# A four-layer graph kernel: its last stage with an early first chunk, a table stored by chunk, and a norm that ends in the ring

## Chip, cores and metric

One core of one Trainium2 chip. The metric is the device time of one execution in microseconds, taken as the median over several runs. A difference of 0.2% (5.5 us) is about the smallest that can be told here.

## The reference, cut to what matters

There are 100000 nodes with 32 features each and 25000 edges, sorted by their target `dst`. Four graph layers follow each other, each as `x = layernorm(x + layer(x))`. The last two are a relation layer (RGCN with attention) and a layer of weighted messages:

```python
nei  = segment_sum(a[:, None] * msg, dst)          # layer 3, msg by edge type
curr = h[src[last_e]] @ self_loop_weight
x = layernorm(x + relu(where(in_deg > 0, nei + curr, 0)))
...
messages = x[src] * edge_attr[:, None]             # layer 4
x = layernorm(x + segment_sum(messages, dst) + x)
```

Layer 3 changes only nodes that are a target of some edge. So the rows `x[dst]` of layer 4 need the new sums everywhere, and the rows `x[src]` only where the source is itself a target.

## The kernel before, in words

Nodes that no edge touches are done in an early phase and stored. The rest is done by edge: the 25000 edges lie on 128 partitions with T = 196 columns each, 32 values in a column. XS holds the value of an edge's source, XD that of its target, both as [128, 196 x 32]. S, Y, SW and YW are work tiles of that size. A chunk is RC = 28 columns (896 values), and there are ROUNDS = 7 chunks; U = 14 columns are half of one.

The stage before the change is the relation layer's group loop (`relation_groups`, L2108). It ends with messages in Y and self-loop terms in S. Everything behind it is what the change touches:

- VectorE sums Y over runs of equal target (32 scans, `sums_of_dst`, L2163), adds Y to S (L2165) and clips at zero (L2166). S is then the table of layer 3, by edge.
- SyncE stores the table to DRAM in one transfer (`write_table`, L722 and L653) and waits for its landing.
- Fetch of listed rows. Edges whose source is itself a target are listed per partition. Of each trip of 8 listed rows (two halves of CU = 4), SyncE moves four indices into `aidx` (L613), GpSimd gathers four times 128 rows from the table into `ring` (`fetch_rows`, L781), and SyncE moves them into YW (L618). The halves alternate. There are seven trips here, 56 gathers. A list row is never ahead of its column: what column t needs lies in list column t or before it.
- VectorE meanwhile adds S to XD and normalizes it by chunk (`norm_chunk`, L1449, called at L2176). It also works out the output rows of the last edge of each run (L2179 to L2184).
- `listed_rows` (L1931, called at L2186) waits for all fetched rows and then spreads them to their columns: eight predicated copies with distances 128 to 1 (`expand`, L1252). Here only distances 128 to 16 are done over the whole tile. The distances 8 to 1 are left to `expand_window` (L2191), which does them for one chunk and the 15 columns before it.
- `out_dst` (L2217) for each chunk: the window, times a 0/1 mask (L2222), added to XS (L2223), norm of XS (`norm_chunk`), times the edge weight (L2225), 32 scans over runs of equal target (L2232) that start from the column before, 2*XD + sums (L2234), a row held for runs that cross partitions (L2236 to L2238), norm of XD. Each norm asks ScalarE for one square root of 28 values (`root`, L1058; `take_roots`, L2266).
- `stepped_ring_pass` (L1158) copies each normalized half chunk and its row numbers into one of two ring slots (`out_fill`, L2211) and signals it. GpSimd scatters it with 14 instructions of 128 rows (`dma_pass`, L483, L493). A slot is filled again when its scatters have landed. The order on VectorE is: chunk, fill slot 0, fill slot 1, next chunk.

An engine runs its instructions in the order of the program. Another engine waits only on semaphores: `s_tabw` (table in DRAM), `s_fst[h]` (32 for each trip of half h, 16 for its rows and 16 for its index move), `s_slot` (a slot is filled), `s_land[h]` (16 for each scatter that landed).

There is a second form of norm, `norm_run` (L1478) with `norm_acts` on ScalarE (L2323). There the squares are ScalarE's, the chunks overlap (center chunk i, scale chunk i-2, variance of chunk i-1), and mean and inverse root lie in PSUM. The two earlier norms of XD use it.

## Time and profile before

| | us |
|---|---|
| median of the timed runs | 2744.0 (three: 2743.14 to 2745.68) |
| the profiled execution, whole | 2745.77 |
| its span from first to last instruction | 2744.0 |
| VectorE busy | 1927.4 (70%) |
| GpSimd busy | 1732.6 (63%) |
| ScalarE busy | 625.0 (23%) |
| TensorE busy, matmul | 533.3 (19%) |

The stage that changes lies in the last 450 us. From 2300 us on TensorE does one small product and its granted clock is 0.50 of full speed (1.2 GHz) throughout, so it has no part here. In the rows, a time is the start from the beginning of the span, and the number behind it the duration; "issue" means that nothing in the profile holds the engine. SPq is the transfer queue of SyncE, where a row is the issue and not the transfer.

### The profile page before, as it was taken

To read this page: it belongs to the slowest core of one execution; us is meant where nothing else is said; L and a number is where in the kernel's file an instruction comes from. 1 tells how busy PE (TensorE), PEld (TensorE's weight loads), DVE (VectorE), ACT (ScalarE), POOL (GpSimd) and SP (SyncE) were. 2 spreads that over 40 slices of the span, in tenths; PEclk is the share of its full clock that TensorE was granted. 3 is DMA by queue.
4 is the path that set the end of the run, shared out by engine and by line. 5 is a ranking of instruction groups with operands and counts; after the bars stand their busy time and mean duration, and the time that the engine had idled before them with its cause. 6 is when DMAs were issued, how large, how long until landed. Compare 5 with 4: busy or idle time off the path is not lost.

```text
span 2744.0 us, 24747 instructions
## 1 busy us (share of the span) xinstructions
PE 533.3 (19%) x3579; PEld 337.4 (12%) x3579; DVE 1927.4 (70%) x3512; ACT 625.0 (23%) x1417; POOL 1732.6 (63%) x1741
## 2 busy tenths in 40 slices
PE   5770000273000000000003032320255550000000
PEld 2330000273000000000003012220122220000000
DVE  7777888888835456546898476059888887587872
ACT  7982233131000000000003013441344430100000
POOL 6777777777567665646657776670566621717776
PEclk9995555597555555555556565555565655555555
DMA  6003333100112122221231201111000001200000
GB/s 229 13 12 91 97 96 100 33 13 13 61 12 34 11 25 28 21 18 72 57 66 22 63 11 9 57 23 48 7 8 8 8 4 52 21 2 10 9 9 9
DMA packets 100894, 101.68 MB, mean 37 GB/s; under 512 B 58169, under 2 KB 92649, under 8 KB 98929
## 3 DMA queue, kind: packets, MB, share of 16 engines
q0 software_dynamic: 53664, 20.91, 8.2%
q1 hardware_dynamic: 46864, 80.15, 8.1%
q14 instruction: 40, 0.32, 0.0%
q10 hardware_dynamic: 320, 0.20, 0.0%
q8 instruction: 6, 0.10, 0.0%
HBM read 38.06 MB, written 60.81 MB: 36 GB/s over the span
## 4 chain that ended last, share of the span: by engine, by line
DVE 36%; issue 21%; POOL 15%; DMA 9%; PE 6%; DVEq 3%; ACT 2%; ACTq 1%; POOLq 1%; SPq 0%
POOL ring L781 6%; POOL cring L477 3%; POOL out_dram L493 3%; DMA cring<-sums_by_list,cidx 2%; PE banks L2746 1%; POOL ring L874 1%; POOL attention_by_edge L881 1%; DVE RB L1259 1%; DVE banks L1100 1%; DVE banks L1090 1%; DVE SW L1096 1%; DVE SW L1095 1%; DVE SW L1105 1%; DVE SW L1383 1%; DVE banks L1084 1%
## 5 line engine op out<-in xcount | busy, mean ns | idle before, releaser
L493 POOL DMA_INDIRECT out_dram<-ring,ridx x196 | 210.3, 1073 | 128.5 <-DVE ridx L2214 68.4
L502 POOL DMA_INDIRECT XS<-in_x_dram,xsi x196 | 199.3, 1017 | 70.0 <-issue 62.2
L502 POOL DMA_INDIRECT SW<-node_table,srci x196 | 200.4, 1022 | 66.1 <-issue 66.1
L502 POOL DMA_INDIRECT XD<-in_x_dram,xdi x196 | 195.4, 997 | 62.7 <-issue 62.7
L900 POOL DMA_INDIRECT out_dram<-z4w,oidx x112 | 111.9, 999 | 126.8 <-ACT oidx L2467 98.1
L477 POOL DMA_INDIRECT cring<-sums_by_list,cidx x128 | 123.8, 967 | 101.7 <-issue 71.0
L2614 PE MATMUL banks<-tl,dcar 128*128 128x32 f32 (+1 forms) x14 | 4.4, 405 | 766.6 <-DVEq L1372 584.1
L2532 PE MATMUL banks<-YW 128*128 128x392 f16 x784 | 139.5, 331 | 46.1 <-ACT YW L2298 45.9
L781 POOL DMA_INDIRECT ring<-x_by_edge,aidx x96 | 102.3, 1066 | 49.6 <-issue 44.8
L781 POOL DMA_INDIRECT ring<-rgcn_table,aidx x56 | 61.8, 1103 | 109.6 <-DMA aidx<-rows 93.4
L2273 ACT ACT_TABLE_LOAD x22 | 28.2, 1283 | 399.7 <-DVEq L1060 399.7
L900 POOL DMA_INDIRECT out_dram<-e4w,oidx x84 | 83.2, 990 | 51.6 <-ACT oidx L2467 27.0
L1003 DVE TENSOR_SCALAR YW<-YW,b_d 128x784 f16<-128x784 f16 x196 | 82.7, 422 | 46.8 <-PE banks L2532 44.9
L2614 PEld LDWEIGHTS banks<-tl,dcar 128*128 128x128 f32 x14 | 3.5, 312 | 769.0 <-DVEq L1372 585.9
L2746 PE MATMUL banks<-w,xw 128*128 128x512 f16 x196 | 92.3, 626 | 0.0
L817 POOL DMA_INDIRECT repeated_edges_by_src<-ring,aidx x64 | 69.5, 1085 | 30.2 <-issue 16.2
L2532 PEld LDWEIGHTS banks<-YW 128*128 128x128 f16 x784 | 73.8, 98 | 112.1 <-issue 65.8
L477 POOL DMA_INDIRECT cring<-sums_by_edge,cidx x56 | 53.0, 946 | 49.1 <-DVE cidx L1574 34.3
L2385 ACT ACTIVATE banks<-xw 128x896 f32<-128x896 f32 x7 | 6.5, 922 | 340.3 <-DVEq L1868 340.3
L1004 DVE TENSOR_SCALAR YW<-YW,b_s 128x784 f16<-128x784 f16 x196 | 82.9, 423 | 0.0
L2291 ACT ACTIVATE YW<-iota_h,a_d 128x128 f16<-128x128 f16 x196 | 76.4, 390 | 6.1
L2121 DVE TENSOR_TENSOR prods<-banks,RB 128x1024 f32<-128x1024 f32 x49 | 60.0, 1224 | 24.9 <-PE banks L2746 24.9
(614 smaller groups left out, 3328.6 us busy)
## 6 DMA issues: line engine op xcount, KB each, us to landing
SW<-in_x_dram SPq DMA_DIRECT2D x20, 625.0 KB
out_dram<-SW SPq DMA_DIRECT2D x20, 625.0 KB
sums_by_list<-RB SPq DMA_DIRECT2D x2, 1800.0 KB
sums_by_edge<-RB SPq DMA_DIRECT2D x1, 3528.0 KB, 9.8
sums_by_list<-RB SPq DMA_DIRECT2D x2, 1600.0 KB
XS<-in_x_dram,xsi POOLq DMA_INDIRECT x196
list_values_by_edge<-RB SPq DMA_DIRECT2D x1, 3136.0 KB
attention_by_edge<-RB SPq DMA_DIRECT2D x1, 3136.0 KB
```

What stands on the lines that cost most here:

```text
L477: pool.indirect_dma_start(out=row, out_offset=None, in_=table, in_offset=off).then_inc(s_lland[v][h], 16)
L493: pool.indirect_dma_start(out=table, out_offset=off, in_=ring_row(h, j, w), in_offset=None, bounds_check=limit, oob_is_err=False).then_inc ...
L502: pool.indirect_dma_start(out=dest[:, t * w:(t + 1) * w], out_offset=None, in_=table, in_offset=bass.IndirectOffsetOnAxis(ap=idx[:, t:t + ...
L781: pool.indirect_dma_start(out=ring_row(h, j, D), out_offset=None, in_=table, in_offset=bass.IndirectOffsetOnAxis(ap=aidx[:, h, j:j + 1], a ...
L817: pool.indirect_dma_start(out=table, out_offset=bass.IndirectOffsetOnAxis(ap=aidx[:, h, j:j + 1], axis=0), in_=ring_row(h, j, w), in_offse ...
L900: pool.indirect_dma_start(out=out[:, :], out_offset=bass.IndirectOffsetOnAxis(ap=oidx[:, j * GT + t:j * GT + t + 1], axis=0), in_=oring_ro ...
L1003: V.tensor_scalar(oh_lo[0][:, j, :], iota_w, col(b_d), None, ALU.is_equal)
L1004: V.tensor_scalar(oh_lo[1][:, j, :], iota_w, col(b_s), None, ALU.is_equal).then_inc(s_oh, 1)
L2121: st.do(V.tensor_tensor(wide_prods[c].rearrange("p (t o b) -> p t o b", t=2, b=NB), pairs[c][:, :].rearrange("p (t o b) -> p t o b", t=2, ...
L2291: last = A.activation(hi_far[:, j, k * P:(k + 1) * P], iota_h[:, 0:P], ACT.Abs, bias=t[:, bass.ds(i * 4 + j, 1)])
L2532: last = M.matmul(bank[2 * k + h][:, 0:HH], oh_hi[b][:, j, k * P:(k + 1) * P], oh_lo[k][:, j, h * HH:(h + 1) * HH], start=False, stop=False)
L2746: M.matmul(bank[c][:, :], x16[:, b, c * P:(c + 1) * P], w16[:, 0:NB * D], start=True, stop=True).then_inc(s_msg, 1)
```

## The change

1. **Table by chunk.** VectorE adds Y to S in seven chunks, each signalled; ScalarE clips each chunk; SyncE stores each as its own transfer. The waits on the table count 16 for each of them.
2. **Norm of XD.** `norm_run` in place of the seven serial `norm_chunk`. Its first operation on a chunk adds S, behind the clip of that chunk.
3. **First chunk early.** When the rows of the first four trips (EARLY) are moved and the next index move has landed, `close_rows` spreads the rows to the first 28 columns, with five distances (16 to 1) in the window alone, and `out_dst` runs for chunk 0. Its result goes, scaled, to z4w and e4w and its row numbers to `oidx` (the buffers of the earlier scatters), and GpSimd scatters 28 times from there. Only then come `listed_rows` with the distances 128 to 16, and chunk 1. The list is padded to at least five trips instead of three (seven are needed here, so nothing changes in that).
4. **The round.** `norm_chunk` is gone. `center` puts the sum in PSUM and subtracts it with the factor -1/32 in one instruction; `deviation` squares, sums, asks for the root and leaves the inverse in PSUM. For XS the inverse is multiplied by the weight first (28 values), so that one product gives the messages and XS itself is not scaled. For XD the last product writes straight into the ring slot (`out_fill`), half by half.
5. **Order of the fills.** In the loop slot 0 is filled at the end of a chunk, and slot 1 behind the window copies of the next chunk, before that chunk's sums.

```diff
+        EARLY = -(-RC // (2 * CU))
...
-            write_table(rgcn_d, 2)
-            sp.wait_ge(s_tabw, 32)
+            for i in range(ROUNDS):
+                sp.wait_ge(s_eo, 3 + i)
+                sp.dma_start(dense(rgcn_d, D)[:, i * (RC * D):(i + 1) * (RC * D)],
+                             S[:, i * (RC * D):(i + 1) * (RC * D)]).then_inc(s_tabw, 16)
+            sp.wait_ge(s_tabw, 16 * (1 + ROUNDS))
             fetch_moves(n0, rows0, YW, s_fst, s_fget, 1)
...
-            pool.wait_ge(s_tabw, 32)
+            pool.wait_ge(s_tabw, 16 * (1 + ROUNDS))
             fetch_rows(n0, rgcn_d[:, :], s_fst, s_fget, 1)
-            dma_pass(pool, PASS_OUT_DST, D, out[:, :], scatter=True, limit=N - 1)
+
+            def scatter_slot(h, row, index):
+
+                for j in range(U):
+                    pool.indirect_dma_start(out=out[:, :], out_offset=bass.IndirectOffsetOnAxis(ap=index(j), axis=0),
+                                            in_=row(j), in_offset=None, bounds_check=N - 1, oob_is_err=False
+                                            ).then_inc(s_land[h], 16)
+
+            pool.wait_ge(s_slot, 2)
+            for h in range(2):
+                scatter_slot(h, lambda j: oring_row((h * U + j) // GT, (h * U + j) % GT),
+                             lambda j: oidx[:, h * U + j:h * U + j + 1])
+            with pool.Fori(0, ROUNDS - 1) as i:
+                for h in range(2):
+                    pool.wait_ge(s_slot, i * 2 + (3 + h))
+                    pool.sem_inc(s_tick[0], 1)
+                    scatter_slot(h, lambda j: ring_row(h, j, D), lambda j: ridx[:, h, j:j + 1])
             pool.wait_ge(s_held, 1)
...
-                st.seq(V.tensor_scalar(trips_i[v][:, :], trips_i[v][:, :], 1 if v else 3, None, ALU.max))
+                st.seq(V.tensor_scalar(trips_i[v][:, :], trips_i[v][:, :], 1 if v else EARLY + 1, None, ALU.max))
...
-            st.seq(V.tensor_tensor(S[:, :], S[:, :], Y[:, :], ALU.add))
-            st.seq(V.tensor_scalar(S[:, :], S[:, :], 0.0, None, ALU.max))
-            dve.sem_inc(s_tab, 1)
-
-            def table_read():
-                dve.wait_ge(s_oslot, NG)
-                dve.wait_ge(s_tabw, 32)
-
-            table_read()
-            with st.loop(ROUNDS, 1 + 8) as i:
+            for i in range(ROUNDS):
+                st.seq(V.tensor_tensor(chunk(S, i), chunk(S, i), chunk(Y, i), ALU.add))
+                dve.sem_inc(s_ei, 1)
+
+            def add_sums(i):
+                dve.wait_ge(s_eo, 3 + i)
                 st.seq(V.tensor_tensor(chunk(XD, i), chunk(XD, i), chunk(S, i), ALU.add))
-                norm_chunk((XD,), i, sq_area=sq_s)
+
+            norm_run(XD, sq_2, add_sums, none)
...
+            def close_rows():
+
+                st.seq(V.tensor_copy(window[:, HALO:, :], Y[:, 0:RC * D].rearrange("p (t d) -> p t d", d=D)))
+                for b in range(CLOSE):
+                    st.do(V.tensor_scalar(near_bit[b][:, HALO:], moved[:, 0:RC], b, 1, ALU.logical_shift_right,
+                                          ALU.bitwise_and))
+                st.wait()
+                for b in range(CLOSE - 1, -1, -1):
+                    n = 1 << b
+                    st.seq(V.copy_predicated(window[:, HALO + n:, :][:, ::-1, :],
+                                             near_bit[b][:, HALO + n:].unsqueeze(2).to_broadcast(
+                                                 [P, RC - n, D])[:, ::-1, :],
+                                             window[:, HALO:HALO + RC - n, :][:, ::-1, :]))
+                return window[:, HALO:, :]
...
+            sq3, half = v3(sq_s[:, 0:RC * D]), roots[:, 0:RC]
+            mean, inv = bank[2][:, 256 + RC:256 + 2 * RC], bank[2][:, 256:256 + RC]
+
+            def center(x3):
+
+                dve.sem_inc(tick, 1)
+                st.seq(V.tensor_reduce(mean, x3, AX.X, ALU.add))
+                st.seq(V.scalar_tensor_tensor(out=x3, in0=bc3(mean, D), scalar=-1.0 / D, in1=x3, op0=ALU.mult,
+                                              op1=ALU.add))
+
+            def deviation(x3):
+
+                st.seq(V.tensor_tensor(sq3, x3, x3, ALU.mult))
+                dve.sem_inc(tick, 1)
+                st.seq(V.tensor_reduce(half, sq3, AX.X, ALU.add))
+                root()
+                st.seq(V.reciprocal(inv, half))
+
+            def add_listed(i, y):
+
+                xs = chunk(XS, i)
+                st.seq(V.tensor_tensor(y, y, cols2(act0, i).unsqueeze(2).to_broadcast([P, RC, D]), ALU.mult))
+                st.seq(V.tensor_tensor(xs, xs, y, ALU.add))
+
+            def out_dst(i, y):
+
                 part = prods[:, :, :].rearrange("p a b -> p (a b)")[:, 0:RC * D].rearrange("p (t d) -> p t d", d=D)
-                over = lambda t: cols2(t, i).unsqueeze(2).to_broadcast([P, RC, D])
                 sums, xs, xd = (chunk(t, i) for t in (S, XS, XD))
-                y = expand_window(i)
-                st.seq(V.tensor_tensor(y, y, over(act0), ALU.mult))
-                st.seq(V.tensor_tensor(xs, xs, y, ALU.add))
-                norm_chunk((XS,), i, sq_area=sq_s)
-                st.seq(V.tensor_tensor(y, xs, over(ew), ALU.mult))
-                if not isinstance(i, int):
+                center(xs)
+                deviation(xs)
+                st.seq(V.tensor_tensor(inv, inv, cols2(ew, i), ALU.mult))
+                st.seq(V.tensor_tensor(y, xs, bc3(inv, D), ALU.mult))
...
+                center(xd)
+                deviation(xd)
+
+            def out_fill(i, h, ago=0):
+
+                x3 = XD[:, bass.ds(i * (RC * D) + (h * U * D - ago * (RC * D)), U * D)].rearrange("p (t d) -> p t d", d=D)
+                V.tensor_tensor(slot(h).rearrange("p (t d) -> p t d", d=D), x3, bc3(inv[:, h * U:(h + 1) * U], D), ALU.mult)
+                V.tensor_scalar(ridx[:, h, :], odi[:, bass.ds(i * RC + (h * U - ago * RC), U)], 0.0, None,
+                                ALU.add).then_inc(s_slot, 1)
+
+            for h in range(2):
+                dve.wait_ge(s_fst[h], trips0 * 32 + 32 * EARLY + 16)
+                dve.sem_inc(tick, 1)
+            dve.wait_ge(s_oslot, NG)
+            dve.wait_ge(s_tabw, 16 * (1 + ROUNDS))
+            y = close_rows()
+            add_listed(0, y)
+            out_dst(0, y)
+            for m in range(len(SLOT_GROUPS)):
+                dve.wait_ge(s_oland[m], 16 * GT * len(SLOT_GROUPS[m]) * ROUNDS)
+            for tile, first, last in ((z4w, 0, 4 * GT), (e4w, 4 * GT, RC)):
+                V.tensor_tensor(tile[:, 0:(last - first) * D].rearrange("p (t d) -> p t d", d=D), XD3[:, first:last, :],
+                                bc3(inv[:, first:last], D), ALU.mult)
+            V.tensor_scalar(oidx[:, :], odi[:, 0:RC], 0.0, None, ALU.add).then_inc(s_slot, 2)
+            listed_rows(2, range(7, NEAR - 1, -1))
+            y = expand_window(1)
+            add_listed(1, y)
+            out_dst(1, y)
+            dve.wait_ge(s_land[0], LAND)
+            out_fill(1, 0)
+            with st.loop(ROUNDS - 2, 2 * NEAR + 54) as k:
+                y = expand_window(k + 2)
+                dve.wait_ge(s_land[1], k * LAND + LAND)
+                dve.sem_inc(tick, 1)
+                out_fill(k + 2, 1, ago=1)
+                add_listed(k + 2, y)
+                out_dst(k + 2, y)
+                dve.wait_ge(s_land[0], k * LAND + 2 * LAND)
+                dve.sem_inc(tick, 1)
+                out_fill(k + 2, 0)
...
-            stepped_ring_pass(PASS_OUT_DST, out_fill(XD, odi), lambda i, h: None, 0, extra=65, before_fill=out_dst,
-                              filled_work=held_row)
+            dve.wait_ge(s_land[1], (ROUNDS - 1) * LAND)
+            out_fill(ROUNDS - 1, 1)
+            held_row()
...
-            take_roots(("norm",), 3 * ROUNDS + 1)
+            for i in range(ROUNDS):
+                part = S[:, i * RC * D:(i + 1) * RC * D]
+                act.wait_ge(s_ei, 3 + i)
+                A.activation(part, part, ACT.Relu).then_inc(s_eo, 1)
+            norm_acts(XD, sq_2)
+            take_roots(("norm",), 2 * ROUNDS + 1)
```

## Rows read from the trace of the kernel before

**Rows 1.** The page, part 4: the chain that ended last, by engine.
```profile
DVE 36%; issue 21%; POOL 15%; DMA 9%; PE 6%; DVEq 3%; ACT 2%; ACTq 1%; POOLq 1%; SPq 0%
```

**Rows 2.** Waits, 2300 to 2744: engine line waited for; us in total, times, longest.
```profile
POOL out_dram L493 <- DVE ridx L2214: 68.4, 7, 64.2
...
DVE banks L1258 <- DMA YW<-ring: 17.1, 1, 17.1
...
DVE ring L2213 <- DMA out_dram<-ring,ridx: 10.8, 6, 2.7
```

**Rows 3.** Timeline, GpSimd, last stage: start, us, engine line op out<-in [idle before, releaser].
```profile
2459.62 1.13 POOL L493 DMA_INDIRECT out_dram<-ring,ridx  x1 [64.24 <-DVE ridx L2214]
...
2621.06 0.98 POOL L493 DMA_INDIRECT out_dram<-ring,ridx  x1 [2.25 <-issue]
...
2698.44 0.99 POOL L493 DMA_INDIRECT out_dram<-ring,ridx  x1 [0.88 <-DVE ridx L2214]
...
2734.51 0.98 POOL L914 DMA_INDIRECT out_dram<-y,cidx  x1 [0.31 <-issue]
```

**Rows 4.** Timeline, VectorE: round 1 of the last stage.
```profile
2500.00 0.88 DVE L2196 COPY RB<-YW 128x1376 f32 x1 [0.20 <-issue]
...
2507.27 1.09 DVE L2222 TENSOR_TENSOR RB<-RB,act 128x896 f32<-128x896 f32 x1
...
2510.97 0.18 DVE L1460 TENSOR_SCALAR roots<-roots 128x28 f32<-128x28 f32 x1
...
2516.94 1.09 DVE L1474 TENSOR_TENSOR XS<-XS,roots 128x896 f32 x1
...
2536.99 0.39 DVE L2213 TENSOR_SCALAR ring<-XD 128x448 f32 x1 [0.26 <-DVE XD L1474]
...
2538.96 0.39 DVE L2213 TENSOR_SCALAR ring<-XD 128x448 f32 x1 [1.37 <-DMA out_dram<-ring,ridx]
```

**Rows 5.** Timeline, GpSimd: one scatter of the same round.
```profile
2517.30 1.58 POOL L493 DMA_INDIRECT out_dram<-ring,ridx  x1 [0.30 <-issue]
```

**Rows 6.** Timeline, all engines: from the table to the first gather.
```profile
2293.52 6.69 DVE L2165 TENSOR_TENSOR SW<-SW,YW 128x6272 f32<-128x6272 f32 x1 [0.31 <-DVE YW L1719]
...
2312.97 1.09 DVE L2175 TENSOR_TENSOR XD<-XD,SW  x1 [9.30 <-DMA rgcn_table<-SW]
...
2315.17 0.99 POOL L781 DMA_INDIRECT ring<-rgcn_table,aidx  x1 [91.11 <-DMA aidx<-rows]
```

**Rows 7.** ScalarE's squares; XD's overlapped norm; the end of the serial one.
```profile
L2329 ACT ACTIVATE RB<-XD x7: 949/951/951, 1347.8 to 1380.9; 128x896 f32<-128x896 f32 x7
...
1344.35 1.09 DVE L1940 SCALAR_TENSOR_TENSOR XD<-XD,SW 128x896 f32<-128x896 f32 x1
...
1388.61 0.07 DVE L1946 MEMSET qi<- 128x8 int32 x1 [0.18 <-DVE XD L1499]
...
2383.12 0.09 DVE L2178 MEMSET y<- 128x32 f32 x1 [0.24 <-DVE XD L1474]
```

**Rows 8.** DMA issues of the whole span: out<-in, queue, KB, us to landing.
```profile
x_by_edge<-xw SPq DMA_DIRECT2D x7, 448.0 KB, 3.7
...
rgcn_table<-SW SPq DMA_DIRECT2D x1, 3136.0 KB, 8.8
```

**Rows 9.** Fetch and first chunk: SyncE, GpSimd, the chain's piece, VectorE.
```profile
2362.69 0.51 SPq L613 DMA_DIRECT2D aidx<-rows  x1
...
2394.43 0.95 POOL L781 DMA_INDIRECT ring<-rgcn_table,aidx  x1 [0.30 <-issue]
...
2394.43 6.28 DMA ring<-rgcn_table,aidx
...
2402.76 0.23 DVE L1258 TENSOR_SCALAR banks<-dsti 128x68 int32<-128x68 int32 x1 [17.05 <-DMA YW<-ring]
...
2424.10 0.63 DVE L2196 COPY RB<-YW 128x896 f32<-128x896 f32 x1
...
2458.23 0.39 DVE L2213 TENSOR_SCALAR ring<-XD 128x448 f32<-128x448 f32 x1
```

More of the change, by code:

```diff
@@ L1156, in rank_batch @@
                 rk.seq(V.tensor_tensor(batch_cols(rpos, i), cnt4[:, :], rk4[:, :], ALU.add))
-            def stepped_ring_pass(n, fill, take, per, round_work=None, extra=0, last_work=None, between=None,
-                                  before_fill=None, next_fill=None, filled=False, landed=None, filled_work=None):
-                if before_fill and not filled:
-                    before_fill(0)
-                if not filled:
-                    for h in range(2):
-                        fill(0, h).then_inc(s_slot, 1)
-                if between:
-                    between()
-                with st.loop(ROUNDS - 1, 2 * per + extra) as i:
-                    if before_fill:
-                        before_fill(i + 1)
-                    for h in range(2):
-                        dve.wait_ge(s_land[h], i * LAND + land_count(n, 0))
-                        dve.sem_inc(tick, 1)
-                        take(i, h)
-                        fill(i + 1, h).then_inc(s_slot, 1)
-                    if round_work:
-                        round_work(i)
-                if filled_work:
-                    filled_work()
-                for h in range(2):
-                    dve.wait_ge(s_land[h], land_count(n, ROUNDS - 1))
-                    dve.sem_inc(tick, 1)
-                    take(ROUNDS - 1, h)
-                    if next_fill:
-                        next_fill(0, h).then_inc(s_slot, 1)
-                if landed:
-                    landed()
-                if last_work:
-                    last_work(ROUNDS - 1)
-            def fill_idx(idx):
-                return lambda i, h: V.tensor_scalar(ridx[:, h, :], cols(idx, i, h), 0.0, None, ALU.add)
             def slot(h, w=D):
@@ L2184, in _ @@
             out_rows(dstf, t3, odi)
-            NEAR = 4
-            listed_rows(2, range(7, NEAR - 1, -1))
+            NEAR, CLOSE = 4, 5
             HALO = (1 << NEAR) - 1
-            near_bit = [bank[1][:, b * 64:b * 64 + HALO + RC].bitcast(I32) for b in range(NEAR)]
+            near_bit = [bank[1][:, b * 64:b * 64 + HALO + RC].bitcast(I32) for b in range(CLOSE)]
             window = RB[:, 2 * RC * D:2 * RC * D + (HALO + RC) * D].rearrange("p (t d) -> p t d", d=D)
-            def expand_window(i):
-                first = isinstance(i, int)
-                lead = HALO if first else 0
-                rows = Y[:, 0:RC * D] if first else Y[:, bass.ds(i * (RC * D) - HALO * D, (RC + HALO) * D)]
-                st.seq(V.tensor_copy(window[:, lead:, :], rows.rearrange("p (t d) -> p t d", d=D)))
-                marks = moved[:, 0:RC] if first else moved[:, bass.ds(i * RC - HALO, RC + HALO)]
+            assert 1 << CLOSE >= RC
@@ L2203, in expand_window @@
                     dve.sem_inc(tick, 1)
-                    at_ = HALO + n if first else HALO + 1 - n
+                    at_ = HALO + 1 - n
                     width = HALO + RC - at_
```

61 lines of the change are left out of this document (8 added, 53 removed).

## Prediction

> **What bounds it now.** The chain of waits runs mostly through VectorE, "issue" gaps and GpSimd [rows 1], so I read where the last 430 us are spent: the table of waits, then the timelines of GpSimd, VectorE and SyncE. The stage after the relation groups has three parts, one after another. First (2293.5 to 2402.8) the table S is added, clipped and stored in one transfer, and only then the seven trips of listed rows are gathered. VectorE normalizes XD meanwhile and then idles 17.1 us for the last rows [rows 2]. Second (2402.8 to 2459.6) VectorE works alone; GpSimd idles 64.2 us before its first scatter [rows 2, 3]. Third, 196 scatters of 128 rows run from 2459.62 to 2734.51, in seven rounds of 28. In the last round VectorE has little left, and a scatter takes (2734.51 - 2698.44) / 28 = 1.288 us, 36.1 a round [rows 3]; the other six take 238.8 (2459.62 to 2698.44), 39.8 each. After the last, 9.5 us follow to the end at 2744.0, which the change doesn't touch.
>
> Why 39.8? Round 1 (the first of the loop) on VectorE: copy at 2500.00, fill of the first half slot at 2536.99, fill of the second at 2538.96 after 1.37 of waiting for a landing, next copy 0.7 later, 39.6 in all [rows 4]. GpSimd has its own delay: a scatter that starts (2517.30) inside a VectorE product with both inputs in SBUF (2516.94, 1.09 long) takes 1.58 instead of 0.98; it is free when the product is [rows 4, 5]. I find about four of these, 0.5 to 0.7 each, in every contended round, so GpSimd alone would need 36.1 + 2.5 = 38.6. The two paces are close, and the landing makes VectorE's the longer one.
>
> **Term 1, table and fetch.** The full add and the clip with the store end at 2312.97, 19.5 after 2293.52; the first gather follows at 2315.17 [rows 6]. Seven adds of 896 columns take 7 x 1.13 = 7.9 (the full add takes 6.7). ScalarE clips each behind its add: it squares 128x896 in 0.95 [rows 7], less than an add, so the last clip is done about 1.1 after the last add. A 448 KB store lands in 3.7 [rows 8], and at 1.13 between issues no store waits: one of seven times the bytes lands in 8.8 [rows 8], so 448 KB more cost 0.85. Last landing: 2293.5 + 7.9 + 1.1 + 3.7 + 0.1 = 2306.3, that is 6.4 earlier; the first gather is at 2308.8. If each store had to end before the next began, 7 x 3.7 instead, it would be 2321.
>
> The norm of XD moves from seven serial chunks (2312.97 to 2383.12, 70.2) to the overlapped form that the kernel already has for XD, with one operation ahead: 1344.35 to 1388.61, 44.3 [rows 6, 7]. It needs no landing any more: 2301.4 + 44.3 = 2345.7, and 2.6 of index work (covered by the fetch) gives 2348.3. All of this gain, 37 us on VectorE, is hidden by the fetch, which is late next; if the fetch were free it would be worth more.
>
> Fetch: 56 gathers took 79.3 from 2315.17 to 2394.43; undisturbed they go at 0.95 + 0.30 = 1.25 [rows 6, 9], 70. The pipelined norm has one two-SBUF product a chunk instead of four, so I take 76 (70 to 80): last gather 2384.8, and the last rows arrive as now 8.3 behind it (the last landing alone is 6.28) [rows 9]: 2393.
>
> **Term 2, the first 28 columns early.** The wait is met when the index moves behind the fourth trip have landed: the later one is issued at 2362.69 [rows 9], about 2 us in flight (the table is in by 2312.97, and the first gather, behind one such move, starts at 2315.17), so 49.5 after the first gather now, 48 then: 2357. VectorE waits 8.7 for it, and the whole fetch before, so this new wait is ahead of nothing that could run. Then the first chunk: from 2424.10 to its fill at 2458.23 it takes 34.1 now [rows 9]. It gains a fifth predicated copy of 384 columns (0.5) and a mark (0.1), and loses 2.8 by term 4: 2357 + 31.9 = 2389. Products into z4w, e4w and an index copy, about 1.7 by length: GpSimd may start at 2391, its fetch having ended at 2386. The 28 early scatters end by 2391 + 38.6 = 2430, under VectorE's next work, so they cost nothing. The waits for the old scatters out of z4w and e4w were met long before: GpSimd has idled 91 us by 2315.17 [rows 6].
>
> **Term 3, what is late next.** After the fill VectorE needs the last rows (2393), then the far steps, 21.3 (2402.76 to 2424.10), unchanged, now between round 0 and round 1; then window, sums and norms of chunk 1. GpSimd idles about 21 us here. A round of VectorE from copy to fill is 37.0 now [rows 4]; after the change:
>
> **Term 4, a round.** Off: two scalings of 28 means (0.2 each with its gap) [rows 4], one 896-column product (1.2, less 0.2 for the small one that replaces it), the last product with its wait (1.35), two extra waits (0.1 each). 37.0 - 0.4 - 1.0 - 1.35 - 0.2 = 34.1. The fills become products of 448 columns, 0.6 each for half of 1.09, and an index copy: about 2.1 for both with gaps. Round: 36.2. Means and inverse roots come from PSUM; the overlapped norm does the same with 1.13 between its steps, so I price that at nothing; bounds -1 to +2. The fill of a second half now waits for its slot behind the window copies, 8 us into the round, when the landing is nearly always past. So VectorE no longer adds its 36.2 to a landing, and GpSimd is the bound. Of the eleven long two-SBUF products of a round six are left, so its delay falls from 2.5 to about 1.4: 37.5. Bounds: 36.1 (none) and 39.8 (as now).
>
> The Trainium skill (SBUF — State Buffer, "Who interferes with whom") says that VectorE with two SBUF inputs contends with a GpSimd instruction that reads SBUF, and that whoever is first holds the shared pair for its whole instruction. The first half fits the stretched scatters; the second doesn't: the product at 2507.27 keeps its 1.09 beside scatters [rows 4]. If VectorE were held too, see rival D.
>
> **The sum.** The last rows are in at 2393; 0.2 of wait and 21.3 of far steps make 2414.5. Chunk 1 from its copy to its fill, 34.1 by term 4, makes 2448.6, the fill 2449.4, and GpSimd's first scatter now starts 0.9 after its fill: 2450.3. Five rounds of 37.5 are 187.5, two pauses of GpSimd like those in the loop now (2.25 before 2621.06 is one) [rows 3] 2.5, the last round 36.1: 2676.4. The held row is ready long before. That is 58 before the 2734.5 of now. The profiled run took 2745.8 in all (span 2744.0) and would take 2687.8; it lies 1.8 above the median of the three timed runs, 2744.0, and that becomes 2686.
>
> **Rivals.**
> A. The pace stays: the 39.8 is GpSimd's own, or PSUM operands cost VectorE 3 us a round. For: the two paces lie 1 us apart. Against: the last, uncontended round. 5 x 2.3 = 11.5: 2697.5.
> B. The stores run one after another: fetch 15 later, all later by that: 2701. Against: the 8.8 for seven times the bytes.
> C. It doesn't do what it says: four trips aren't free of the rest (a wait on the whole fetch, or the moves queue behind). The first chunk starts at 2393 instead of 2357, and VectorE's chain grows by the 34 of the first chunk: 2720. Against: moves are issued trip by trip [rows 9].
> D. VectorE held by scatters: six products, met 3 times in 4, by half a scatter: 2.2 a round, 38.4, 0.9 past GpSimd's 37.5: 2690.5. It lies in my range.
> E. Slower. The wait for the second half's landing stands in the middle of a round with 29 us of work and the next first fill behind it. It starts to cost when a landing takes over 37.5 - 30.2 = 7.3 us, and eats all of the gain when it takes 58 / 5 = 11.6 more, 18.9; at 21 the time is 2754. Landings now leave waits of 10.8 in six [rows 2], the longest seen is 6.28 [rows 9]. So only a queue that backs up behind the early scatters does it.
>
> **How the numbers follow.** Forecast with D 0.80, A 0.10, B 0.04, C 0.04, E 0.02. The time is the forecast's, 2686. The range: fetch at its bounds (+-4), rounds at 36.9 to 38.6 (-3, +5.5), VectorE's chain -2 to +3, not all at once, gives 2676 to 2695; taking in A and B, 2676 to 2702. A measurement can tell 0.2%, 5.5 us, from no change. Faster 0.97, same 0.01, slower 0.02.
>
> **What will show it.** The first scatter of the last stage near 2391, the first gather near 2309, a GpSimd gap of 20 to 25 us after 28 scatters, then 37.5 a round with no wait on the fill, fewer scatters over 1.3 us; VectorE idle 8 to 10 before the fifth predicated copy, a chunk's loop of 36 without waiting on ScalarE for more than the root. A gap before each round's first scatter would speak for A or D; a first gather after 2315 for B; a first chunk after 2390 for C; VectorE waiting on landings over 5 us for E.

## Result and profile after

| | before | after |
|---|---|---|
| median of the timed runs, us | 2744.1 (four: 2743.1 to 2745.7) | 2681.45 (four: 2680.0 to 2684.1) |
| profiled execution, us | 2745.8 | 2680.0 |
| its span, us | 2744.0 | 2678.3 |

The ratio is 0.9772, 95% interval 0.9755 to 0.9789: 62.6 us less. The forecast was 2686, its range 2676 to 2702.

In the two profiled executions the stage begins at 2293.52 before and 2290.42 after (start of the first add of Y to S); those 3.1 us lie ahead of everything that the change touches. All stage times below are counted from that add.

| from the add, us | before | forecast | after |
|---|---|---|---|
| first gather | 21.7 | 15.3 | 14.6 |
| last gather | 100.9 | 91.3 | 90.4 |
| first chunk: window copy | 130.6 | 63.5 | 60.6 |
| first scatter | 166.1 | 97.5 | 92.4 |
| far steps begin | 109.2 | 99.7 | 96.8 |
| scatters of the second chunk begin | 204.8 | 156.8 | 150.3 |
| last scatter (held row) | 441.0 | 382.9 | 378.3 |

The profile after, the page's first part:

```profile
PE 535.2 (20%) x3579; PEld 338.8 (13%) x3579; DVE 1902.7 (71%) x3483; ACT 611.2 (23%) x1410; POOL 1721.3 (64%) x1741
```

VectorE is busy 24.7 us less and GpSimd 11.3 less, both under the 62.6 that the kernel gained: most of it is work that now overlaps. The waits from 2290 us on (engine line waited for; total, times, longest) answer to [rows 2]:

```profile
DVE ring L2200 <- DMA out_dram<-ring,ridx: 27.6, 4, 11.5
POOL out_dram L894 <- DVE ridx L2201: 22.4, 7, 20.6
...
DVE banks L2164 <- ACT roots L2268: 9.3, 14, 0.7
```

GpSimd's 64.2 us wait for the first fill has become 20.6. VectorE's waits for landings grew from 10.8 to 27.6, and a wait for a root is 0.7 long (9.3 in fourteen) where it was 1.9 (25.2 in thirteen, over the scatters of before). The table and the fetch, in the timeline of all engines (start, duration):

```profile
2290.42 8.52 DVE L2093 TENSOR_TENSOR SW<-SW,YW 128x896 f32<-128x896 f32 x7 [0.31 <-DVE YW L1646]
...
2292.57 7.76 SPq L699 DMA_DIRECT2D rgcn_table<-SW  x7
...
2299.09 1.09 DVE L2098 TENSOR_TENSOR XD<-XD,SW 128x896 f32<-128x896 f32 x1
...
2305.01 0.99 POOL L759 DMA_INDIRECT ring<-rgcn_table,aidx  x1 [83.43 <-DMA aidx<-rows]
```

The seven stores are issued behind the clips, about 1.2 apart, and the first gather starts 14.6 after the first add ([rows 6]: 21.7). VectorE in the first two chunks and the beginning of the loop:

```profile
2351.00 0.63 DVE L2117 COPY RB<-YW 128x896 f32<-128x896 f32 x1 [5.16 <-DMA aidx<-rows]
...
2364.68 0.34 DVE L2164 RECIPROCAL banks<-roots 128x28 f32<-128x28 f32 x1 [0.66 <-ACT roots L2268]
...
2387.17 0.23 DVE L1212 TENSOR_SCALAR banks<-dsti 128x68 int32<-128x68 int32 x1 [5.21 <-DMA YW<-ring]
...
2439.10 0.62 DVE L2200 TENSOR_TENSOR ring<-XD,banks 128x448 f32<-128x448 f32 x1
...
2439.71 0.87 DVE L2133 COPY RB<-YW 128x1376 f32 x1
...
2473.02 0.98 DVE L2133 COPY RB<-YW 128x1376 f32 x1
```

The first chunk waits 5.16 for the fourth trip and the far steps 5.21 for the last rows. From one window copy to the next (2439.71 to 2473.02) a round of VectorE that waits for no landing takes 33.3. GpSimd's scatters:

```profile
2382.79 1.01 POOL L894 DMA_INDIRECT out_dram<-z4w,oidx  x1 [1.01 <-DVE oidx L2217]
...
2440.68 0.98 POOL L894 DMA_INDIRECT out_dram<-ring,ridx  x1 [20.60 <-DVE ridx L2201]
...
2558.27 0.98 POOL L894 DMA_INDIRECT out_dram<-ring,ridx  x1 [1.63 <-issue]
...
2668.75 0.98 POOL L908 DMA_INDIRECT out_dram<-y,cidx  x1 [0.30 <-issue]
```

After 2440.68 GpSimd is never again kept waiting by VectorE; the one pause left (1.63) has no releaser. Five rounds take 192.0, the last 36.0.

### The profile page after: what moved, and what is told of

The parts are those of the page before. It is cut to its first block, busy times and chain, and to the rows that moved or that the text cites. A ratio compares the mean times of both kernels' runs of the same rounds, so it can differ in the third digit from the quotient of the medians.

```text
span 2678.3 us, 24492 instructions
## 1 busy us (share of the span) xinstructions
PE 535.2 (20%) x3579; PEld 338.8 (13%) x3579; DVE 1902.7 (71%) x3483; ACT 611.2 (23%) x1410; POOL 1721.3 (64%) x1741
## 4 chain that ended last, share of the span: by engine, by line
DVE 37%; issue 20%; POOL 15%; DMA 8%; PE 6%; DVEq 3%; ACT 2%; ACTq 1%; POOLq 0%; SPq 0%
POOL ring L759 6%; POOL cring L467 3%; POOL out_dram L894 2%; DVE RB L1213 2%; DMA cring<-sums_by_list,cidx 2%; POOL attention_by_edge L859 2%; PE banks L2746 2%; POOL ring L852 1%; DVE banks L1094 1%; DVE banks L1084 1%; DVE SW L1090 1%; DVE SW L1099 1%; DVE SW L1089 1%; DVE SW L1337 1%; DVE banks L1078 1%
## 5 line engine op out<-in xcount | busy, mean ns | idle before, releaser
L894 POOL DMA_INDIRECT out_dram<-ring,ridx x168 | 175.6, 1045 | 72.8 <-issue 50.4
L759 POOL DMA_INDIRECT ring<-x_by_edge,aidx x96 | 100.5, 1047 | 48.9 <-issue 44.3
L795 POOL DMA_INDIRECT repeated_edges_by_src<-ring,aidx x64 | 70.5, 1102 | 30.2 <-issue 16.2
L2286 ACT ACTIVATE YW<-iota_h,a_s 128x128 f16<-128x128 f16 x196 | 75.6, 386 | 0.0
```

The costliest lines, as they stand in the source:

```text
L759: pool.indirect_dma_start(out=ring_row(h, j, D), out_offset=None, in_=table, in_offset=bass.IndirectOffsetOnAxis(ap=aidx[:, h, j:j + 1], a ...
L795: pool.indirect_dma_start(out=table, out_offset=bass.IndirectOffsetOnAxis(ap=aidx[:, h, j:j + 1], axis=0), in_=ring_row(h, j, w), in_offse ...
L894: pool.indirect_dma_start(out=out[:, :], out_offset=bass.IndirectOffsetOnAxis(ap=index(j), axis=0), in_=row(j), in_offset=None, bounds_che ...
L2286: last = A.activation(hi_far[:, j, k * P:(k + 1) * P], iota_h[:, 0:P], ACT.Abs, bias=t[:, bass.ds(i * 4 + j, 1)])
```

## Experiments

The forecast gave every gain to a place. The first four kernels test the places one by one; the rest ask what a round of 28 scatters costs, the step in which the trace and the forecast disagree most. The theory at the start was the forecast's; its main rival A says that the pace is GpSimd's own. Medians are given with the ratio to the kernel before in the same batch and its 95% interval. The changed kernel was timed in one batch, 2681.45; its interval touches those of the variants from 2675 to 2688 below, and there the stage times of the profiled executions decide. They repeat better than the medians: the start of the stage varies from 2289.0 to 2295.1 over the fourteen profiles, while the changed kernel and two variants with the same loop (whole fetch, one store) take 192.0 for their five rounds, all three.

**One load of the square root's table ahead of the kernel before's last stage.** In ScalarE's timeline of before a root (second row below) has a table load ahead of it each time; after the change one load stands at 2306.99 and none ahead of the roots that follow:

```profile
2514.80 1.28 ACT L2273 ACT_TABLE_LOAD   x1 [20.58 <-DVEq L1060]
2516.09 0.34 ACT L2273 ACTIVATE roots<-roots,eps_norm 128x56 f32<-128x56 f32 x1
```

```profile
2488.43 0.34 ACT L2268 ACTIVATE roots<-roots,eps_norm 128x56 f32<-128x56 f32 x1 [16.82 <-DVEq L1054]
```

```diff
+            A.activation(all_roots[0], all_roots[1], ACT.Sqrt)
             take_roots(("norm",), 3 * ROUNDS + 1)
```

> The kernel before, with one square root on ScalarE ahead of its last loop and nothing else, so that the loop should need no function table load for each root. Theory: a load of 1.28 us lies in each root of the last stage, on VectorE's path. Of the 21 in the chunks, the 7 of the serial norm of XD hide under the fetch; the 2 of chunk 0 are on the path (2.6); in the rounds VectorE's 39.6 falls by 2.6 to below GpSimd's own 38.6, so only about 1.1 of it counts, five or six times. Together 8 to 9 us: 2735. Rival 1: VectorE sets the pace of all of it, 14 x 1.28 = 18: 2726. Rival 2: the loads are hidden: 2744.

Measured: 2741.0 (0.9988, 0.9978 to 0.9997), stage end (the last scatter, counted from the add as in the table) 438.8 instead of 441.0. VectorE's root wait fell from 1.9 to 0.7, so its round is 2.6 shorter, yet the rounds still take 39.66, 39.68, 39.65. Waits of VectorE in the stage, and two scatters in GpSimd's timeline:

```profile
DVE ring L2213 <- DMA out_dram<-ring,ridx: 26.2, 6, 5.2
DVE roots L1472 <- ACT roots L2273: 8.0, 12, 0.7
```

```profile
2529.70 1.59 POOL L493 DMA_INDIRECT out_dram<-ring,ridx  x1 [0.31 <-issue]
...
2535.47 1.45 POOL L493 DMA_INDIRECT out_dram<-ring,ridx  x1 [0.31 <-issue]
```

What VectorE gained it gave to waiting for landings (10.8 to 26.2), while GpSimd waited for no fill. So 39.65 is GpSimd's own pace, and VectorE's was level with it: the forecast's reading of before (GpSimd alone 38.6, VectorE's landing makes it 39.6) falls. The 2.2 at the stage end are 1.7 ahead of the first scatter and 0.5 in six rounds; the time fell by 3.6 where 8 to 9 had been expected.

**Stores by chunk and the overlapped norm alone, in the kernel before.** The diff is that of parts 1 and 2 of the change; as `norm_acts` comes with them, the table loads go too.

> The kernel before with parts 1 and 2 of the change alone (table by chunk, overlapped norm of XD); the first chunk comes after the whole fetch, with the old rounds. Theory: the fetch starts 6 to 8 earlier and runs 2 to 3 faster, the norm's own 26 us are hidden by it, and the table loads are gone as in the run before (8.5): 2744 - 18 = 2726. Rival: the norm's time on VectorE counts too: 2700 to 2705.

Measured: 2726.9 (0.9941, 0.9924 to 0.9957). First gather 14.6 from the add, second chunk's scatters at 188.7 instead of 204.8, rounds 39.8 as before. 16.1 of the 17 us lie ahead of the second chunk's scatters: the far steps begin 12.8 earlier (96.4 for 109.2), and the first chunk is 2.5 shorter from its window copy to its scatter, the two roots without a table load. Again the rounds don't feel that VectorE is faster.

**The first chunk waits for the whole fetch, in the changed kernel.**

```diff
-                dve.wait_ge(s_fst[h], trips0 * 32 + 32 * EARLY + 16)
+                dve.wait_ge(s_fst[h], trips0 * 64)
```

> The changed kernel, but chunk 0 waits for all seven trips of listed rows instead of four. Theory: VectorE's chain from the last rows to the first fill of round 1 grows by the whole of chunk 0, 31 us: 2681 + 31 = 2712. Rival: GpSimd's 20.6 us of idle behind round 0 takes most of it up, so only 10: 2692.

Measured: 2711.7 (0.9883, 0.9866 to 0.9899), 30.2 more. The first scatter (GpSimd's timeline) and its wait:

```profile
2419.01 1.01 POOL L894 DMA_INDIRECT out_dram<-z4w,oidx  x1 [37.71 <-DVE oidx L2217]
```

VectorE's whole first chunk stands on the path again, and the second chunk's scatters start at 180.9, 30.6 later. That is the price of rival C.

**One store, in the changed kernel.**

```diff
-            for i in range(ROUNDS):
-                sp.wait_ge(s_eo, 3 + i)
-                sp.dma_start(dense(rgcn_d, D)[:, i * (RC * D):(i + 1) * (RC * D)],
-                             S[:, i * (RC * D):(i + 1) * (RC * D)]).then_inc(s_tabw, 16)
+            sp.wait_ge(s_eo, 2 + ROUNDS)
+            sp.dma_start(dense(rgcn_d, D), S[:, :]).then_inc(s_tabw, 16)
...
```

> The changed kernel with the table clipped by chunk but stored in one transfer behind the last clip. Theory: the store lands 8.8 after its issue instead of about 2.5 to 3, so the fetch and all behind it come 6.4 later: 2687.5. Rival: VectorE's waits of 5.2 before chunk 0 and before the far steps show that the fetch isn't alone on the path, and 1 to 2 of it is hidden: 2686. Rival 2: no difference, 2681.

Measured: 2688.2 (0.9798, 0.9782 to 0.9815), 6.7 more; first gather at 21.4 from the add (+6.8), last scatter +6.6. The fetch passes a delay on in full, as the sum assumed.

From before to after this makes three steps: stores, norm and table loads 17.2; the early first chunk 30.2; and 15.2 between (2726.9 less 2711.7), which is a remainder and was not tested by itself. It is more than the new round: of the 16.0 between the two stage ends (424.9 and 408.9), 7.8 lie ahead of the second chunk's scatters (180.9 for 188.7), since in the kernel that waits for the whole fetch the far steps already run beside the first chunk's scatters, and 8.2 in the rounds from there on.

**Table loads back in the changed kernel**, by a Tanh on unused values behind each root, so that the next root has to load its table again:

```diff
-            take_roots(("norm",), 2 * ROUNDS + 1)
+            def other_set(k):
+                A.activation(all_roots[0], all_roots[1], ACT.Tanh).then_inc(s_other, 1)
+                act.wait_ge(s_other, k + 1)
+                act.sem_inc(tick, 1)
+
+            take_roots(("norm",), 2 * ROUNDS + 1, other_set)
```

> The changed kernel with the table loads put back: behind each root ScalarE does a small tanh of unused values, so that every root loads its table again (1.28 us). Theory: of two loads a chunk those of chunk 0 are hidden by the wait for the last rows (5.2), those of chunk 1 are on the path (2.6), those of the rounds hidden, since VectorE's 33.3 become 35.9 and GpSimd takes 38.2: 2681 + 2.6 = 2684. Rival: VectorE sets the pace, 12 x 1.28 = 15: 2697.

Measured: 2685.2 (0.9789, 0.9773 to 0.9805), stage end +4.1, of it 3.4 ahead of the second chunk's scatters and 0.6 in the five rounds. VectorE's 2.6 more a round are hidden in the loop.

**Means and inverse roots in SBUF instead of PSUM, in the changed kernel**, so that nine long and two half products of a round have both inputs in SBUF:

```diff
-            mean, inv = bank[2][:, 256 + RC:256 + 2 * RC], bank[2][:, 256:256 + RC]
+            mean, inv = all_roots
```

> The changed kernel with mean and inverse root of the last stage in SBUF instead of PSUM; instructions, shapes and order stay. Theory: five more VectorE instructions of a round (two subtractions, the product to messages, two fills) then have both inputs in SBUF, and scatters that start inside them are stretched: 1.0 to 1.5 a round for GpSimd, 5 to 7 in all: 2687. VectorE's own durations stay at 1.09. Rival 1: the place doesn't matter: 2681. Rival 2: VectorE is held as well, its instructions grow to 1.5 or more and its round passes 38: 2692 or more.

Measured: 2686.1 (0.9792, 0.9775 to 0.9808), stage end +5.8: the fetch 2.3 longer (its gathers run beside the first chunk), the five rounds 2.9. The sum is near the expected 5 to 7, but not by the expected way: a round grew by 0.6, not by 1.0 to 1.5, and the rest came from the fetch, which I had not counted.

**Slot 1 filled ahead of the window copies; and that with the table loads.**

```diff
-                y = expand_window(k + 2)
                 dve.wait_ge(s_land[1], k * LAND + LAND)
                 dve.sem_inc(tick, 1)
                 out_fill(k + 2, 1, ago=1)
+                y = expand_window(k + 2)
```

> The changed kernel with the second half slot filled ahead of the next window instead of behind it, as in the kernel before. Theory: VectorE's round with the landing (33.3 + 3) still is below GpSimd's 38.2: no change, 2681 +- 1. Rival: the order of the fills is what took the landing off the path, the pace goes back to about 39.6: 2688.

> Both of the two before: second slot filled ahead of the window, and table loads put back. Theory: VectorE's 35.9 and the landing of 2.7 and its fill, about 39.4, now pass GpSimd's 38.2: 1.2 in four or five rounds, and 2.6 in chunk 1: 2689. If the effects only add (2.6 + 0), 2684.

Measured: 2683.3 (0.9784, 0.9767 to 0.98) and 2687.3 (0.98, 0.9784 to 0.9816), stage ends +2.8 and +5.1. The second took the same rounds as the first to 0.02 us (38.65, 38.64, 39.92 against 38.67, 38.64, 39.94). The interaction that I expected, a VectorE that becomes the bound once both are there, does not exist at this size: with about 36 of work (33.3 and 2.6 of loads) in a round of 38.6 it has slack either way. The second median, 2687.3, lies nearer to the 2689 of my theory than to the 2684 of mere addition, but the rounds don't bear the theory out. The order of the fills is worth 2.8 at the stage end (1.0 ahead of the second chunk's scatters, 1.7 in the five rounds); the medians alone can't tell that from nothing.

**Two masks of the changed kernel in PSUM**, so that four of six long products keep both inputs in SBUF:

```diff
+            act0p, heldp = bank[0][:, 0:T], bank[0][:, T:2 * T]
+            st.do(V.tensor_scalar(act0p, act0[:, :], 0.0, None, ALU.add))
+            st.seq(V.tensor_scalar(heldp, held[:, :], 0.0, None, ALU.add))
```

> The changed kernel, with two small masks of the last stage (act0 and held, 196 columns each) copied once to PSUM, so that two of the six long products of a round no longer have both inputs in SBUF. VectorE issues the same products. Theory G (five rounds of scatters are paced by GpSimd, whose scatters are stretched by those products): each round loses about 0.4 us of stretch, the five rounds together about 2 to 2.5, so about 2679.0 where the changed kernel takes 2681.5. Theory V (VectorE's round or the landings set the pace): no difference, 2681.5.

Measured: 2682.6 (0.9774, 0.9758 to 0.9791), five rounds 192.6 instead of 192.0. A miss for theory G as I had it, and the timelines show why. First the changed kernel, GpSimd and then VectorE:

```profile
2481.59 1.56 POOL L894 DMA_INDIRECT out_dram<-ring,ridx  x1 [0.31 <-issue]
2483.45 0.98 POOL L894 DMA_INDIRECT out_dram<-ring,ridx  x1 [0.30 <-issue]
...
2486.03 1.85 POOL L894 DMA_INDIRECT out_dram<-ring,ridx  x1 [0.30 <-issue]
```

```profile
2481.21 1.09 DVE L2169 TENSOR_TENSOR RB<-RB,act 128x896 f32<-128x896 f32 x1
2482.43 1.09 DVE L2170 TENSOR_TENSOR XS<-XS,RB 128x896 f32 x1
...
2485.93 1.09 DVE L2160 TENSOR_TENSOR RB<-XS 128x896 f32 x1
```

A scatter that starts inside such a product ends 0.86 after the product does: 2481.21 + 1.09 + 0.86 = 2483.16 (2481.59 + 1.56 = 2483.15), and 2485.93 + 1.09 + 0.86 = 2487.88, within 0.01 both. In the last stages of all fourteen profiles, 293 scatters of the 310 that start over 0.13 before such a product's end, end 0.85 to 0.87 behind it. In the other 17 the scatter starts up to 0.05 behind the product's start, keeps its 0.98, and the product is the one that grows, to 1.13 to 1.17. One of them, from the kernel before:

```profile
2467.48 1.15 DVE L2223 TENSOR_TENSOR XS<-XS,RB 128x896 f32 x1
2467.51 0.98 POOL L493 DMA_INDIRECT out_dram<-ring,ridx  x1 [0.30 <-issue]
```

Of products with an operand in PSUM none is longer than 1.09, and all 150 scatters that start inside one keep 0.98 or 0.99. Now the sheltering. In the changed kernel's rows the product between the two scatters (2482.43) starts while the first scatter runs and ends at 2483.52, 0.07 after the next scatter has started, and that one keeps its 0.98: it costs nothing. Now the kernel with the masks in PSUM, one round:

```profile
2454.09 1.25 POOL L894 DMA_INDIRECT out_dram<-ring,ridx  x1 [0.30 <-issue]
...
2456.93 1.90 POOL L894 DMA_INDIRECT out_dram<-ring,ridx  x1 [0.30 <-issue]
```

```profile
2452.17 1.08 DVE L2172 TENSOR_TENSOR RB<-RB,banks 128x896 f32<-128x896 f32 x1
2453.39 1.09 DVE L2173 TENSOR_TENSOR XS<-XS,RB 128x896 f32 x1
...
2456.88 1.09 DVE L2163 TENSOR_TENSOR RB<-XS 128x896 f32 x1
```

The mask product holds nobody up any more, but now the scatter behind it meets the next one, XS + RB, which had been free in the shadow of the first. Of products in a chain about every second one is paid for, so taking one out moves the bill to its neighbour.

**Masks in PSUM and the squares on ScalarE**, so that two products are left (XS + RB, 2*XD + sums):

```diff
-                st.seq(V.tensor_tensor(sq3, x3, x3, ALU.mult))
+                dve.sem_inc(s_q2w, 1)
+                dve.wait_ge(s_q2r, n)
...
+                    act.wait_ge(s_q2w, 2 * i + m + 1)
+                    A.activation(sq_s[:, 0:RC * D], t[:, i * RC * D:(i + 1) * RC * D], ACT.Square).then_inc(s_q2r, 1)
+                    take_roots(("norm",), 1)
```

> As the one with two masks in PSUM, and the two squares of each round are made by ScalarE, so that only two long products of a round (xs + y and 2 xd + sums) still have both inputs in SBUF. Two semaphore trips to ScalarE a round, about the length of the product that they replace. Theory G: each round loses about 1.1 to 1.5 us of stretch against the changed kernel and comes to 37.0 or less, five rounds 6 to 7: 2675. Theory V: no difference from the changed kernel, 2681.5, or slower if the trips to ScalarE cost VectorE more than its slack of about 4 us a round.

Measured: 2675.0 (0.9751, 0.9734 to 0.9767), 6.4 under the changed kernel's median; stage end 372.1, 6.2 earlier; the five rounds 185.1, 7.0 less. The two intervals touch, but no timed run of either reaches the other's (2673.5 to 2677.7 against 2680.0 to 2684.1), and each round of the profile is 1.1 to 1.5 shorter. This version beats both kernels. Waits of VectorE in the rounds, and a scatter and the instruction of VectorE that it met:

```profile
DVE ring L2205 <- DMA out_dram<-ring,ridx: 21.2, 4, 10.2
```

```profile
2474.50 1.64 POOL L895 DMA_INDIRECT out_dram<-ring,ridx  x1 [0.30 <-DVE ridx L2206]
```

```profile
2474.41 0.88 DVE L2137 COPY RB<-YW 128x1376 f32 x1 [0.21 <-issue]
```

The window copy has one input, and the scatter waits for it all the same: 2474.41 + 0.88 + 0.86 = 2476.15, against 2474.50 + 1.64 = 2476.14. I had counted products with two inputs in SBUF alone. Here VectorE waits too, which I had overlooked. In the changed kernel's loop:

```profile
2543.79 0.98 POOL L894 DMA_INDIRECT out_dram<-ring,ridx  x1 [0.31 <-issue]
...
2544.34 0.43 DVE L2201 TENSOR_SCALAR ridx<-etyi 128x14 int32 x1
2544.44 1.04 DVE L2133 COPY RB<-YW 128x1376 f32 x1
```

The index copy, 0.17 otherwise, ends with the scatter (2544.77), and the window copy, 0.88 otherwise, ends 0.72 behind it. A window copy that starts up to 0.55 after a scatter goes first instead, and the scatter ends 0.12 behind the copy: in the kernel before with the table loaded, the copy below (the scatter at 2535.47 above, 1.45 long) makes 2535.92 + 0.88 + 0.12 = 2536.92 = 2535.47 + 1.45.

```profile
2535.92 0.88 DVE L2196 COPY RB<-YW 128x1376 f32 x1 [0.20 <-issue]
```

**The kernel before with its small operands in PSUM, without and with the loaded table.** They ask whether the finding holds where the forecast had misread it:

```diff
-                st.seq(V.tensor_scalar(roots[:, 0:k * RC], roots[:, 0:k * RC], 1.0 / D, None, ALU.mult))
+                st.seq(V.tensor_scalar(small[:, 0:k * RC], roots[:, 0:k * RC], 1.0 / D, None, ALU.mult))
...
-                st.seq(V.reciprocal(roots[:, 0:k * RC], roots[:, 0:k * RC]))
+                st.seq(V.reciprocal(small[:, 0:k * RC], roots[:, 0:k * RC]))
...
+            act0p, heldp, ewp = bank[0][:, 0:T], bank[0][:, T:2 * T], bank[3][:, 0:T]
+            for to, of in ((act0p, act0), (heldp, held), (ewp, ew)):
+                st.do(V.tensor_scalar(to, of[:, :], 0.0, None, ALU.add))
```

In both, the copy of the edge weights lies where the far steps put their marks afterwards, so the messages of layer 4 are weighted by those marks. Instructions, shapes and row numbers are the same, and so the time can be read.

> The kernel before, with the small operands of the last stage in PSUM: mean, inverse root and the three masks act0, held and ew. VectorE issues the same instructions in each round, but only four of its eleven long products (xs + y, 2 xd + sums, two squares) have both inputs in SBUF. Theory G (the 39.65 of a round before is GpSimd's own, 36.1 and about 3.6 of stretch): the stretch falls to about 1.3, GpSimd alone would need 37.4, and VectorE's round of about 38.2 with its landing becomes the bound, so 38.4 a round, six rounds 6 to 7 less: 2737. Theory V (the 39.65 is VectorE's round plus the landing that it waits for): no difference from the kernel before, 2743.5.

> The kernel before with both: small operands in PSUM, and ScalarE's table of the square root loaded once ahead of the stage, so that VectorE's round is 2.6 shorter. Theory G: neither bound is left at 39.65, GpSimd's 37.4 sets the pace, 2.2 less in each of six rounds, and 2 more ahead of the first scatter: 2743.5 - 13.2 - 2 = 2728. If what is worth 3.5 us alone (the loaded table) and the small operands simply add up: 2733.5. Theory V: as with the loaded table alone, 2740.

Measured: 2740.6 (0.999, 0.998 to 0.9999) and 2731.2 (0.9949, 0.9933 to 0.9966); stage ends 435.9 and 427.9, against 441.0 before and 438.8 with the loaded table alone. The waits of VectorE for a landing, in the first and in the second:

```profile
DVE ring L2218 <- DMA out_dram<-ring,ridx: 4.9, 5, 2.1
```

```profile
DVE ring L2218 <- DMA out_dram<-ring,ridx: 15.4, 6, 3.4
```

And how GpSimd waits for the fill in the first:

```profile
2531.95 1.52 POOL L493 DMA_INDIRECT out_dram<-ring,ridx  x1 [1.52 <-DVE ridx L2219]
```

Fewer stretched scatters alone turn GpSimd's stretch into a wait for VectorE's fill; a faster VectorE alone turns into waits for landings; both together shorten the round to 37.8. The six rounds become 5.2 and 0.5 shorter with either alone (small operands, loaded table) and 12.1 with both; at the stage end 5.1, 2.2 and 13.1. That is more than the sum, as it must be when two bounds lie at the same height. The first takes 38.9 a round where I had reckoned 38.4, and the time of the second is nearer to the sum of the parts (2733.5) than to my 2728.

All the rounds close in one account. From GpSimd's timeline, means of the contended rounds (six for the kernels of before, five after), with stretch = what the 28 durations have over 0.98 and pauses = what their gaps have over 0.305:

| kernel | round | stretch | pauses | rest |
|---|---|---|---|---|
| before | 39.80 | 2.97 | 0.85 | 35.98 |
| before, table loaded | 39.71 | 3.45 | 0.28 | 35.98 |
| before, small operands in PSUM | 38.94 | 1.43 | 1.53 | 35.98 |
| before, both | 37.78 | 1.39 | 0.42 | 35.97 |
| after | 38.41 | 2.12 | 0.30 | 35.99 |
| after, statistics in SBUF | 39.00 | 2.72 | 0.30 | 35.98 |
| after, slot 1 first | 38.75 | 2.45 | 0.31 | 35.99 |
| after, masks in PSUM | 38.52 | 2.23 | 0.31 | 35.98 |
| after, masks and squares | 37.01 | 0.70 | 0.33 | 35.98 |

28 scatters cost 28 x 1.285 = 35.98, and everything above it is stretch or a pause. A pause of 1.3 more than the 0.305 stands once in each kernel, with no releaser, and in all fourteen profiles ahead of the same scatter, the 114th of the 196. So it goes with a place in GpSimd's own sequence, whatever VectorE does.

## Why the prediction was right, and where not

**Term 1** held. First gather at 14.6 for 15.3, fetch 75.8 for 76, the norm of XD 44.1 for 44.3 and hidden. The far steps began 2.9 early: the last rows came 6.4 behind the last gather, not 8.3.

**Term 2** held: the early chunk started 2.9 before its forecast (VectorE waited 5.2 for it, not 8.7), and the experiment that takes it away loses 30.2, near the 34 of rival C. Its length was 31.8 from copy to first scatter for 34.

**Term 3** held to 0.5: GpSimd idles 20.6, the far steps take 21.3.

**Term 4, VectorE's part, was mis-sized**: 33.3 for 36.2. Of this, 2.6 are the two table loads of each chunk. They stood in the trace of before, a load ahead of each root, and `norm_acts`, which the change puts ahead of the loop, leaves the square root's table in place. I had costed that call for its squares alone. In the sum it counts once, in the second chunk, which ran 3.5 shorter; in the loop it is hidden, as the kernel with the loads put back shows (+0.6 in five rounds).

**Term 4, GpSimd's part, failed as a reading and missed by 0.6 as a number.** "GpSimd alone would need 36.1 + 2.5 = 38.6" and "the landing makes VectorE's the longer one" are wrong: with VectorE relieved, rounds stay at 39.65 with no wait for a fill. The two bounds of before were level, and the premise of rival A (the pace is GpSimd's own) was true, though not its conclusion, since the change lowers this pace. From there I scaled: eleven products to six, 2.5 to 1.4, round 37.5. Measured were 2.97 to 2.12, round 38.1 without the pause. Three things are behind it. The forecast counted about four stretched scatters a round; before there are four to six, 0.6 each on average (and up to 0.9), and six in most rounds once VectorE is relieved. Products that follow one another shelter each other, so the cost doesn't go with their number: eleven of them stretch five scatters a round, six of them still four. And the window copy hits too. Five rounds, with the single pause of 1.3 for the 2.5 allowed, came to 192.0 for 190.0.

**The sum**: the second chunk's scatters 6.5 early (2.9 of the last rows, 3.5 of the chunk), the rounds 2.0 late, in all 4.6 early: 2681.5 for 2686. Two misses of opposite sign hid each other in part, so some of the closeness of the total is luck.

**Rivals.** A: 2697 did not come, nor do operands in PSUM cost VectorE anything (those products take 1.08 or 1.09). B: the stores overlap, 14.6. C: 2711.7 when forced. D: VectorE is held, but hardly: products that start more than 0.05 before or after a scatter's start keep 1.08 or 1.09, those that start together with one take up to 1.17, and the window copy takes up to 1.05 for 0.88. None of this costs time, since VectorE has slack in the loop; the forecast's 2.2 a round is far above it. The Trainium skill (SBUF — State Buffer, "Who interferes with whom") says that the shared ports are an exclusive lock, and of VectorE's fast two-port modes that whoever issues first has the pair for the whole instruction and the other is fully blocked; the forecast took the last part for products too. These rows show the lock both ways. VectorE's instructions hold the scatter for their whole length, but the scatter holds VectorE only for a part of its own: the products near its start, the copies near its end. The same section also counts copies in their fast modes among those that contend, which the window copy's rows bear out (1376 values in 0.88, where a product takes 1.09 for 896), and which the forecast had not used. E: landings. I had named waits over 5 us as its sign; they came (11.5 the longest) and cost nothing, since GpSimd was never without a full slot. The right sign would have been a gap of GpSimd, not a wait of VectorE.

Left open: what the pause of 1.3 ahead of the 114th scatter is, why the last rows come 6.4 behind the last gather instead of 8.3, and how the 15.2 of the remainder divide between the new round, the order of the fills and the far steps that move behind the first chunk.

## What to carry to other kernels

When two engines hand slots to each other and their paces lie within a microsecond, a trace hardly says which is the bound: the waits go to whichever is ahead, and relieving one of them on the chip tells. Expect less from either alone (here 0.5 and 5.2 in six rounds) than from both (12.1), and look for a change that relieves both. Cost contention by what a chain of operations leaves uncovered, not by counting the operations: here two products fewer brought nothing and four fewer 1.4 us a round. And for each call that a change adds on ScalarE, look at which function's table it leaves loaded for what follows.

## What the runs showed of the hardware

- An indirect scatter of 128 rows takes 0.98 and 0.305 between. If it starts inside a VectorE product with both inputs in SBUF (1.09), or inside the window's copy (0.88), it ends 0.86 after that instruction's end: 1.25 to 1.90 in the rows shown. If the window's copy starts up to 0.55 after the scatter, the scatter ends 0.12 after the copy (1.45).
- The scatter holds VectorE too, for a short part: a product that starts within 0.05 of the scatter's start takes up to 1.17, later ones keep their 1.09; an index copy (0.17) or a window copy (0.88) that starts late in a scatter (0.55 and 0.65 after its start in the rows shown) waits for its end and takes 0.43 and 1.04.
- With the mean or inverse in PSUM the same product (1.09) stretches no scatter (150 met, 0.98 or 0.99).
- A load of ScalarE's table takes 1.28 and stood ahead of every root of the loop, though only one function runs in it; one earlier use of that function removed all 22 of them (fifteen from the first chunk on).
- With seven stores of 448 KB, issued 1.2 apart, the first gather starts 6.8 us earlier than with one of 3136 KB behind the last clip (14.6 for 21.4 from the add).
